# Bringing the expert rows of the second batch's last seven tiles back to their tokens by matrix products instead of gathers, in an attention and mixture-of-experts block

## The reference

```
q = _ln(latents, ...);  x = latents + _mha(q, q, ...)
x = x + _mha(_ln(x, ...), _ln(tokens, ...), ...)
h = _ln(x, ln_g, ln_b)
logits = h @ rw.T + rb
vals, idx = jax.lax.top_k(logits, 2)
gates = jax.nn.softmax(vals, axis=-1)
h1 = gelu(einsum('nd,efd->enf', hf, fc1_w) + fc1_b[:, None, :])     # 128 -> 512
eo = einsum('enf,edf->end', h1, fc2_w) + fc2_b[:, None, :]          # 512 -> 128
gathered = eo[idx_f, jnp.arange(N)[:, None], :]
mixed = (gathered * gates_f[..., None]).sum(axis=1)
return x + mixed
```

## Time and profile before

| | |
|---|---|
| device time, median of 3 | 272.69 us |
| device time of the profiled execution | 272.78 us |
| its span in the profile | 270.8 us |
| TensorE busy | 248.6 us (92%) |
| VectorE busy | 184.0 us (68%) |
| ScalarE busy | 162.2 us (60%) |
| GpSimd busy | 61.6 us (23%) |
| mean traffic of the DMA queues | 72 GB/s |

### The profile page before, as it was taken

How to read it: one execution, slowest core, us unless ns; L and a number is a source line. 1 busy time by engine, 2 the same in 40 slices (tenths; PEclk the granted TensorE clock), 3 DMA queues, 4 the chain that set the end, 5 groups by cost and what they waited for, 6 DMA issues and landing times.

```text
span 270.8 us, 5195 instructions
## 1 busy us (share of the span) xinstructions
PE 248.6 (92%) x1699; PEld 141.1 (52%) x1699; DVE 184.0 (68%) x369; ACT 162.2 (60%) x289; POOL 61.6 (23%) x110
## 2 busy tenths in 40 slices
PE   6899999999999999899999999998999999999540
PEld 2354533433333433345453455334699999999430
DVE  3859689999989889567554499764377455455543
ACT  3383465676776879869676413871576776766300
POOL 3560000000022020000222020175105700036372
PEclk9999999999999999999999999999999999999955
DMA  7107131240322220530110310013302261122232
GB/s 238 43 9 282 68 90 44 69 113 18 87 65 84 80 80 2 165 114 0 28 61 5 87 32 5 4 50 93 86 19 61 74 189 41 31 59 61 68 87 69
DMA packets 18634, 19.37 MB, mean 72 GB/s; under 512 B 2805, under 2 KB 15025, under 8 KB 18609
## 3 DMA queue, kind: packets, MB, share of 16 engines
q1 hardware_dynamic: 15089, 10.36, 13.2%
q10 hardware_dynamic: 2496, 6.59, 7.6%
q0 software_dynamic: 1024, 2.10, 2.7%
HBM read 9.13 MB, written 5.51 MB: 54 GB/s over the span
## 4 chain that ended last, share of the span: by engine, by line
PE 78%; DVE 9%; issue 3%; POOL 3%; ACT 2%; DMA 2%; POOLq 1%; DVEq 0%; ACTq 0%
PE ps_o L1108 11%; PE ps_r L1184 10%; PE ps_r L1175 10%; PE ps_r L1088 9%; PE ps_o L971 7%; PE ps_r L1046 6%; PE ps_x L946 3%; PE ps_r L982 3%; DVE row_max L808 2%; PE ps_o L1120 2%; PE ps_x L971 2%; PE ps_r L1058 2%; PE ps_o L1115 2%; PE ps_x L975 2%; ACT probs L654 2%
## 5 line engine op out<-in xcount | busy, mean ns | idle before, releaser
L654 ACT ACTIVATE probs<-ps_r 128x1024 f32<-128x1024 f32 (+1 forms) x88 | 83.6, 984 | 26.1 <-PE ps_r L1088 23.2
L804 DVE TENSOR_REDUCE row_max<-ps_r 128x2 f32<-128x1024 f32 x64 | 76.0, 1222 | 13.4 <-PE ps_r L1046 11.9
L704 ACT ACTIVATE parts<-ps_r,staged 128x128 f32<-128x128 f32 x120 | 33.2, 379 | 17.2 <-PE ps_r L1175 16.0
L1108 PE MATMUL ps_o<-probs,v_aug 128*9 128x512 f32 x256 | 33.3, 594 | 0.0
L541 POOL CAST max_part<-row_max 128x16 fp32r<-128x16 f32 x16 | 3.1, 196 | 128.9 <-issue 92.8
L971 PE MATMUL ps_o<-ones_bf 128*128 128x512 bf16 x114 | 32.4, 382 | 0.0
L1175 PE MATMUL ps_r<-rows_T,staged 128*128 128x128 f32 x240 | 30.8, 277 | 0.5 <-DVE staged L893 0.5
L1046 PE MATMUL ps_r<-k_tile,q_tile 32*128 32x512 f32 x128 | 29.9, 480 | 0.9 <-ACT probs L654 0.7
L1184 PE MATMUL ps_r<-staged,parts 128*128 128x128 f32 x240 | 30.7, 275 | 0.0
L1088 PE MATMUL ps_r<-q_tile,k_tile 32*128 32x512 f32 x128 | 29.3, 484 | 1.5 <-ACT probs L654 1.0
L808 DVE TENSOR_REDUCE row_max<-ps_r 128x4 f32<-128x616 f32 x32 | 24.3, 794 | 8.1 <-PE ps_r L1058 7.8
...
...
## 6 DMA issues: line engine op xcount, KB each, us to landing
...
```

Source lines behind the costliest of these rows:

```text
L654: nc.scalar.activation(probs[:, i:i + w], ps_r[:, slot("s", r), 0:w], ACT.Exp, scale=SCALE).then_inc(s_read, 1)
L704: ins = nc.scalar.activation(hidden[:, n % HIDDEN, c], ps_r[:, slot("s", r), 0, c * P:c * P + P], ACT.Gelu, bias=staged[:, o % STAGES, 2 * ...
L804: nc.vector.tensor_reduce(heads[:, 2 * pair:2 * pair + 2, t], ps_r[:, slot("m", r)], AX.X, ALU.max).then_inc(m_read, 1)
L1108: mm = nc.tensor.matmul(ps_o[32 * j:32 * j + DH + 1, :], v_aug[:, b, c, 4 * g + j], probs[:, region(n) + j], start=first, stop=last, tile_ ...
```

## The change

`BACK = 7`: the last seven tiles of the second batch (`fc2:23` to `fc2:29`) are no longer written to DRAM and gathered. Instead:

- **Marks.** Each (token, expert) pair of the second batch writes two numbers, the token's number and the gate, to its place in a DRAM array `marks_at` (`mark`, 8 indirect DMAs of 8-byte rows on GpSimd). SyncE waits for all of them and reads the marks of the last seven tiles (`load_marks`).
- **Gate rows.** With the token numbers 0 to 511 in each partition (`numbers`, a broadcast load on ScalarE's queue; the array of marks and the row of zeros are cleared there in the step `zero`, too), VectorE makes for each of the seven tiles a 128x512 matrix with the gate of a place at its token's column (`gate_rows`, one `tensor_scalar`).
- **Back.** TensorE multiplies that with the tile's 128 rows, four 128x128x128 products a tile that accumulate in `ps_o` (`back`). VectorE adds the bank to the output in four pieces (`sum`).
- **Gathers.** Those of the second batch wait for its first eight tiles only, and take their index from `near_of`, the place capped at 1,024, where a row of zeros lies.
- **What moves.** `b2:0`, `gT:1`, `b2:1`, `gates:1` and the first batch's gathers, `comb` and `store` steps move up among the tiles. The exponential of `gates:1` moves to GpSimd as a power of e (`exp`). Saves 9 to 14 come behind `load_marks` on SyncE.

```
+BACK = 7
+LAST = B * TILES - BACK
+FAR = (TILES - BACK) * P
...
-    fc2:20 fc1:22 stage:24 fc2:21 save:10
+    save:3 stage:9 gates:1 fc1:7 fc2:6 stage:10 ... load_rows:1 mark:0 load_marks:0 fc2:11
+    ... fc2:14 save:9-14 ... xT:5 b2:0 fc2:16 gather:0 ... fc2:29 back:5-6 comb:4 comb:5 comb:6 comb:7
+    sum:4 store:4 sum:5 store:5 sum:6 store:6 sum:7 store:7
...
+        numbers = x_hat[:, :, :].rearrange("p t d -> p (t d)")
+        back = probs[:, 0:BACK]
...
+                elif kind == "load_marks":
+                    sp.wait_ge(marked, 16 * TOP * QT)
+                    sp.dma_start(place_marks[:, :, :], marks_at[FAR:TILES * P, :].rearrange("(j p) c -> p j c", p=P)) \
+                        .then_inc(marks_loaded, 16)
...
+                elif kind == "exp":
+                    pool.wait_ge(logits_shifted, ORDER["router", n] + 1)
+                    link(nc.gpsimd.memset(growth[:, :, :], math.e))
+                    nc.gpsimd.tensor_tensor(expd[:, n], growth[:, :, :], shifted[:, n], ALU.pow).then_inc(growth_ready, 1)
+                elif kind == "mark":
+                    pool.wait_ge(marks_cleared, 32)
+                    pool.wait_ge(marks_ready, 1)
+                    for t in range(QT):
+                        pool.wait_ge(m_filled, M_RING["fc2", 8 + 2 * t] + 1)
+                        for k in range(TOP):
+                            nc.gpsimd.indirect_dma_start(
+                                marks_at, bass.IndirectOffsetOnAxis(place_of[:, 1, k, t:t + 1], 0),
+                                marks[:, k, t], None).then_inc(marked, 16)
                 elif kind == "gather":
-                    pool.wait_ge(rows_stored[b], 16 * TILES)
+                    pool.wait_ge(rows_stored[b], 16 * (TILES - BACK if b else TILES))
                     if b:
                         pool.wait_ge(combined, ORDER["comb", t] + 1)
+                        pool.wait_ge(near_ready, 1)
+                        pool.wait_ge(marks_cleared, 32)
                     else:
-                        pool.wait_ge(m_filled, M_RING["fc2", TILES + 2 + 3 * t] + 1)
+                        pool.wait_ge(m_filled, M_RING["fc2", TILES + 1 + 2 * t] + 1)
...
+                    act.dma_start(marks_at.rearrange("(p j) c -> p (j c)", p=P), o_raw[:, 1, 0:2 * TILES]) \
+                        .then_inc(marks_cleared, 16)
+                    act.dma_start(places_out[1][FAR:FAR + 1, :], o_raw[0:1, 1, 0:D]).then_inc(marks_cleared, 16)
+                elif kind == "numbers":
+                    act.wait_ge(misc_filled, MISC_USE["hT", x_hats[-1]] + 1)
+                    act.dma_start(numbers, rows[N_ROWS:N_ROWS + S].partition_broadcast(P)).then_inc(numbers_loaded, 16)
...
+                    if n:
+                        nc.vector.tensor_scalar(near_of[:, :, :], chosen_place[:, :, :], float(FAR), None, ALU.min) \
+                            .then_inc(near_ready, 1)
...
+                    if n:
+                        nc.vector.tensor_copy(marks[:, :, :, 0], cols_sb[:, C_TOKEN:C_TOKEN + QT].unsqueeze(1)
+                                              .to_broadcast([P, TOP, QT]))
+                        nc.vector.tensor_copy(marks[:, :, :, 1], gate_of[:, n]).then_inc(marks_ready, 1)
...
+                elif kind == "gate_rows":
+                    if n == 0:
+                        dve.wait_ge(marks_loaded, 16)
+                        dve.wait_ge(numbers_loaded, 16)
+                        dve.wait_ge(pv_done, SELF_PV + 2 * B * G)
+                    nc.vector.tensor_scalar(back[:, n], numbers, place_marks[:, n, 0:1], place_marks[:, n, 1:2],
+                                            ALU.is_equal, ALU.mult).then_inc(back_ready, 1)
+                elif kind == "sum":
+                    t = n % QT
+                    dve.wait_ge(brought_back, BACK)
+                    dve.wait_ge(combined, ORDER["comb", n] + 1)
+                    nc.vector.tensor_tensor(x_out[:, 1, t], ps_o[:, t * D:t * D + D], x_out[:, 1, t], ALU.add) \
+                        .then_inc(summed, 1)
...
+                elif kind == "back":
+                    j = LAST + n
+                    pe.wait_ge(back_ready, ORDER["gate_rows", n] + 1)
+                    pe.wait_ge(rows_ready, ORDER["fc2", j] + 1)
+                    if n == 0:
+                        pe.wait_ge(o_copied, 2 * B * G)
+                    for t in range(QT):
+                        mm = nc.tensor.matmul(ps_o[:, t * D:t * D + D], back[:, n, t * P:t * P + P], rows_out[:, 1, j - TILES],
+                                              start=(n == 0 and t == 0), stop=(n == BACK - 1), skip_group_check=True)
+                    mm.then_inc(brought_back, 1)
```

More of the change, by code:

```diff
@@ L41 @@
 C_CROSS = C_LOW + 2
[L42 removed]
+C_TOKEN = C_CROSS + 1
+N_COLS = C_TOKEN + S // P
 TOP = 2
@@ L95 @@
[L95 to L103, removed]
-    fc1:23-24 stage:25 save:11 fc2:22 fc1:25 save:12 xT:7 save:13 stage:26 save:14-15 fc2:23 stage:27 fc1:26 save:16
@@ L105 @@
-    fc2:24 stage:28 gather:1 fc1:27 fc2:25 gather:2 save:17-18 stage:29 save:19 fc1:28 save:20 fc2:26 fc1:29
-    save:21-22 fc2:27 save:23 fc2:28 save:24 gather:0 gather:3 save:25 fc2:29 save:26-29 b2:0 comb:1 gather:5 comb:2
-    comb:0 store:2 gather:7 comb:3 gates:1 gT:1 gather:4 b2:1 store:3 store:0-1 comb:5 comb:7 comb:4 gather:6
-    store:7 comb:6 store:5 store:4 store:6
+    warm:1 pv:39 q:3 scores:72 pv:38 oc:11 numbers:0 scores:71 oT:9 scores:70 pv:37 oT:11 pv:36 warm:2 max:80 oc:10
@@ new lines @@
+    oT:10 max:83 max:81 warm:2 max:85 warm:1 osT:2 warm:1 max:82 neg:12 max:86 proj:2 warm:5 mT:12 ln:4 max:84
+    max:87 max:90 hat:4 warm:3 max:95 neg:13 warm:5 mT:13 max:88 max:91 warm:3 hT:4 max:89 warm:2 max:93 warm:2
+    router:0 scores:81 rank:0 scores:79 neg:14 warm:5 mT:14 scores:80 max:92 pv:43 max:94 neg:15 scores:77 prefix:0
+    scores:76 scatter:0 words:0 pv:42 oc:13 mT:15 scores:78 scatter:1 scores:84 scores:83 warm:1 pv:40-41 oT:13
+    gates:0 oc:12 scores:82 stage:0 warm:1 scores:86 scatter:2-3 scores:85 pv:45 pv:44 load_rows:0 oc:14 scores:87
@@ new lines @@
+    stage:1 oT:12 stage:2 pv:46 oT:14 pv:47 stage:3 oc:15 oT:15 warm:5 osT:3 warm:2 proj:3 warm:3 gT:0 ln:5 hat:5
+    warm:6 xT:0 warm:3 hT:5 fc1:0 router:1 exp:1 fc1:1-2 rank:1 fc2:0 xT:1 fc2:1 save:0 fc1:3 stage:4-5 prefix:1
+    fc1:4-5 scatter:5 save:1 scatter:4 fc2:2 xT:2 stage:6 fc2:3 stage:7 fc2:4 stage:8 fc1:6 scatter:7 save:2 fc2:5
+    save:3 stage:9 gates:1 fc1:7 fc2:6 stage:10 fc1:8 fc2:7 stage:11 scatter:6 fc1:9-10 save:4 xT:3 fc2:8-9 save:5
+    fc1:11 stage:12-13 save:6 fc2:10 save:7 fc1:12 stage:14 save:8 words:1 load_rows:1 mark:0 load_marks:0 fc2:11
@@ new lines @@
+    fc1:13 stage:15 fc1:14 fc2:12 xT:4 stage:16 fc2:13 stage:17 fc2:14 save:9-14 fc1:15-17 stage:18 fc2:15 stage:19
+    xT:5 b2:0 fc2:16 gather:0 stage:20 fc1:18 fc2:17 fc1:19 stage:21 fc2:18 gather:1 fc1:20 stage:22 gT:1 fc1:21
+    xT:6 fc2:19 comb:0 stage:23 b2:1 fc2:20 gather:2 gate_rows:0 fc1:22 stage:24 fc2:21 comb:1 fc1:23-24 stage:25
+    save:15-19 fc2:22 gather:3 gate_rows:1 fc1:25 save:20-22 store:0-1 xT:7 stage:26 fc2:23 comb:2 gate_rows:2
+    stage:27 fc1:26 fc2:24 gather:4 stage:28 gate_rows:3 fc1:27 back:0 fc2:25 comb:3 gather:5-7 stage:29 store:2-3
@@ L109 @@
+    gate_rows:4 fc1:28 back:1 fc2:26 gate_rows:5 fc1:29 back:2 fc2:27 gate_rows:6 back:3 fc2:28 back:4 fc2:29
+    back:5-6 comb:4 comb:5 comb:6 comb:7 sum:4 store:4 sum:5 store:5 sum:6 store:6 sum:7 store:7
 """
@@ L295, in build @@
         chosen_place = sb("chosen_place", [P, TOP, QT])
+        near_of = sb("near_of", [P, TOP, QT], I32)
+        marks = sb("marks", [P, TOP, QT, 2])
+        place_marks = sb("place_marks", [P, BACK, 2])
+        growth = sb("growth", [P, QT, E])
         rows_in = sb("rows_in", [P, B, TILES, D])
@@ L679, in _ @@
                     act.dma_start(fc_sb[:, n], fc_w[:, n]).then_inc(fc_loaded, 16)
-                elif kind == "gates":
+                elif kind == "gates" and n == 0:
                     act.wait_ge(logits_shifted, ORDER[step] + 1)
```

36 lines of the change are left out of this document (23 added, 13 removed).

## The result

| | before | changed |
|---|---|---|
| device time, median of 15 | 272.69 us | 274.76 us |
| lowest to highest | 272.24 to 274.19 | 273.11 to 276.59 |
| ratio, 95% interval | | 1.0063, 1.0042 to 1.0085 |
| profiled execution: device time, span | 272.78, 270.8 us | 275.4, 273.7 us |
| last `fc2` ends, in the profile | 253.0 us | 266.3 us |

The change does what it says, and is 2.1 us (0.6%) slower. The forecast was 272.4 us with a range to 275.0: the time lies in the range, near its upper end, and "no change" was the wrong call. The median hides that the 15 runs form three groups. Six take 273.1 to 273.6 us, seven 274.7 to 275.4, two 276.6.

What follows compares the result with a forecast made beforehand. TensorE was taken as the bound until the last `fc2`, then a 17.8 us tail. Shortening the tail gains 10.5 us, work added on TensorE costs 10.1: 272.4 us, no change, from 271.5 to 273.4, 8-in-10 range 270.2 to 275.0.

Steps and rivals of the forecast that it cites:

- `b2:0`, wait and neighbours: On TensorE behind `xT:5`: 0.89 us of products plus 1.01 us standing still until ScalarE frees `ps_x`, together 1.90.
- `stage:27`: Weights staged on VectorE behind `comb:2` and `gate_rows:2`: ready after 3.36 us, TensorE has 2.68 until `fc1:27`; wait 0.68.
- `gates:1`: VectorE's gate work ahead of `stage:10`: 1.8 us against 0.9 of room before `fc1:10`, so TensorE stands 0.9 us.
- `gT:1` with `xT:6`: On TensorE, `gT:1` one `fc1` ahead of `xT:6`: turns of 0.44 us and a 0.55 wait for `ps_x`, together 0.99.
- `b2:1` with its neighbour: On TensorE one `fc2` behind `xT:6`: 0.89 us plus a 0.50 wait while ScalarE finishes its copies, together 1.39.
- ahead of the first tile: Before the tiles: clears on ScalarE's queue lie in its idleness, `numbers` costs 0 to 0.6 us; taken as 0.
- TensorE never stands idle for long there, so I take the full clock.: For the `back` steps ahead of `fc2:29` on TensorE: 0.89 us each at full clock, five making 4.46 us.
- The smaller waits: Rival, 20 in 100: TensorE's waits for `gates:1`, `stage:27` and `ps_x` shrink by 0.9, 0.7 and 0.5; some 270.3 us.
- Saves behind the marks: Rival, 14 in 100: on SyncE saves 9 to 14 land late behind `load_marks`, stopping VectorE at `comb:0`; 273.4 to 275 us.
- `exp` and the ports: Rival, 10 in 100: GpSimd's 3.6 us power holds VectorE's `rank:1` comparisons out of SBUF; +3.4 us, 275.8 us.
- The gathers stay last: Rival, 3 in 100: second-batch gathers, expected landed at 262 against 265.8 wanted, come 4 us late; each beyond costs 1 us.
- Gate rows: Each `gate_rows` on VectorE, 512 columns, takes 0.54 us, between a floor of 0.28 and a ceiling of 0.70.

Runs made afterwards that it cites:

- e2: Changed kernel in its own order with filler products on TensorE ahead of all five waiting steps; 273.51 us.
- e9: Changed kernel with four filler products only in front of `b2:0`, the other four pauses kept; 273.63 us.
- e3: Changed kernel with `gates:1` set behind `stage:11` instead of `stage:9`; 275.15 us (272.43 to 279.88).
- e4: Changed kernel with `comb:4` to `comb:6` moved up among the last copies, only `comb:7` left behind the last; 271.94 us, ratio to before 0.9988.
- e8: Changed kernel with `gates:1` behind `stage:11` and `xT:4` one product later, behind `fc2:13`; 274.59 us.
- e11: e6 with five tiles returned by products instead of seven (`BACK = 5`); 271.69 us.
- e5: Changed kernel with `stage:27` ahead of `comb:2` and `gate_rows:2` on VectorE, `gate_rows:2` behind `stage:28`; 274.3 us.
- e12: e6 with `b2:0` set back right behind `xT:5`; 271.47 us.
- e7: Kernel before with only `b2:0` moved to behind `xT:5`, no back products and no marks; 273.79 us.
- e6: Changed kernel with turning-buffer steps apart, `gates:1` and `xT:4` later, `stage:27` first, `comb:4` to `comb:6` earlier; 269.08 us, ratio to before 0.9869.

## Why the prediction was wrong

The large terms were right. The tail is 7.4 us for a forecast of 7.26, the combs 3.12 for 3.06, a step of `back` 0.89 as forecast. What failed is on TensorE ahead of the last `fc2`: 13.26 us came on, 10.1 were forecast. By differences of starts in the two timelines, in the profiled run with its one fall:

| term | forecast | profile |
|---|---|---|
| granted clock behind the pause | 0 | 1.59 |
| `b2:0`, wait and neighbours | 1.90 | 2.22 |
| `stage:27` | 0.68 | 1.09 |
| `gates:1` | 0.9 | 0.75 |
| `gT:1` with `xT:6` | 0.99 | 1.01 |
| `b2:1` with its neighbour | 1.39 | 1.46 |
| five `back` | 4.46 | 4.46 |
| small waits for weights | -0.2 | +0.14 |
| ahead of the first tile | 0 | 0.54 |
| sum | 10.1 | 13.26 |

- **The failed step is "TensorE never stands idle for long there, so I take the full clock."** The same text had counted 1.01 us of standing still ahead of `b2:0`. That pause costs itself (0.87 us by its row, 1.03 by the starts) and, where the clock falls behind it, 1.6 us more for products at half clock. Nine of the 15 runs of the changed kernel have a fall, and with a filler in the pause (e2, e9) 0 of 16; what is shown is that for this kernel filling the pause takes the falls away. Why only a part of the executions falls stays open. The Trainium skill, TensorE: Matmul & The Clock Gate, Part 1 (The HAM clock gate), says that the gate follows how busy the array has been recently; the trace agrees at this place, 1.00 ahead of the pause and 0.62 behind it, and fillers keep it at 1.00 in e9.
- **Without a fall** the changed kernel takes 273.26 us (median of six), still 0.6 above before and 0.9 above the forecast. Beside the fall the profile shows 1.57 us too many: 0.54 ahead of the first tile, and sizes: `b2:0` 0.3, `stage:27` 0.4, small waits 0.3. (The time around the span was 1.7 us, not 1.98, which takes 0.3 off again; no undisturbed run of this kernel was profiled.) At `b2:0` the wait was right, 1.03 by the starts for 1.01; its own products took 1.09 us for 0.89 and its neighbour 0.1 more. For `stage:27` the count lacked that a `comb` starts 0.2 us behind an eviction, and that the copy of the weights took 0.86 us, not 0.70. A gather ran beside it, but one ran beside the copy at 250.29 as well, and that took 0.69:

```profile
252.25 0.35 DVE L995 SCALAR_TENSOR_TENSOR x_sb<-o_tok,gate_of,x_sb 128x128 f32<-128x128 f32 x1 [0.23 <-ACT rows_T L742]
252.64 0.35 DVE L998 SCALAR_TENSOR_TENSOR x_sb<-o_tok,gate_of,x_sb 128x128 f32<-128x128 f32 x1
253.03 0.55 DVE L983 TENSOR_SCALAR probs<-x_hat,place_marks 128x512 f32<-128x512 f32 x1
253.49 0.86 DVE L947 COPY staged<-fc_sb 128x1028 f32 x1
```

- **The 0.54 us ahead of the tiles** were forecast at nothing, and their cause stays open. At 121 us TensorE waits for a small DMA in the profiles of the changed kernel, e3, e4, e8 and e11:

```profile
121.25 0.50 PE L1162 MATMUL ps_r<-q_tile,k_tile 32*128 32x512 f32 x2 [0.28 <-DMA q_tile<-max_rows]
```

  But e5 and e12 are as late without that wait. `fc1:0` starts at 193.97 us in the profile of before and at 193.85 in e7, and at 194.06 to 194.48 in all profiles with the change, apart from e3 with its two falls. So a part of it may well be the change's own; no run takes `numbers` or the clears out.

- **The smaller waits** (20 in 100) did not come: each wait was there. By the starts they are 1.03 us ahead of `b2:0` (forecast 1.01), 0.52 ahead of `xT:6` (0.55), 0.28 ahead of `b2:1` (0.50), 0.75 for the gates (0.9) and 1.09 ahead of `fc1:27` (0.68). The one for the gates is of another kind than forecast: 0.50 of it stands ahead of `fc1:9`, released by VectorE's semaphore step L977 behind the copy of `fc2:6`, which had to wait behind the gates, and only the rest ahead of `fc1:10`. The 2.77 us that the forecast takes until `ps_x` is free are 2.83 by its own terms (1.10, 1.14 and 0.59), which changes nothing here. That this wait disappears does not free its time either, as e3 and e8 show.
- **Saves behind the marks** (14 in 100): no. `gather:0` starts at 237.06, when the last save has landed, and `comb:0` waits for no DMA at 243.09, nor at 241.22 in e9, which has no fall. The time of this rival, 273.4 to 275, was met by another cause.
- **`exp` and the ports** (10 in 100): no. The power ran right beside the comparisons of `rank:1`, and each took 0.42 us, as in the profile of before:

```profile
197.33 0.42 DVE L892 TENSOR_TENSOR beats<-logit 128x256 f32<-128x256 f32 x1
...
199.03 0.42 DVE L896 TENSOR_REDUCE rank<-beats 128x32 f32<-128x256 f32 x1
```

```profile
197.74 5.62 POOL L585 TENSOR_TENSOR expd<-growth,shifted 128x32 f32<-128x32 f32 x1
```

  So these rows go with the row at 11.36 of the earlier trace rows. The Trainium skill, SBUF — State Buffer, section Who interferes with whom, has VectorE instructions with two SBUF inputs and a GpSimd instruction that reads SBUF contend; this trace does not agree, 0.42 us each beside the power. The power itself took 5.62 us for my 3.6: (5.62 - 1.04) / 28 = 0.16 us a column beyond four, where the step from two columns to four had given 0.09. It was hidden all the same, to 203.4, with the gates at 211.2.
- **The gathers stay last** (3 in 100): not in this order. They are next in line: a `comb` waits 0.25 us for them in e6 and 1.56 in e11.
- **Gate rows**: 0.54 to 0.55 us, the value taken.
